# Two head groups whose cross-attention tiles alternate in the last batch of a decoder layer

## The reference

```python
x = x + self_attention(layernorm(x))          # 16 heads of 32, q and k layer-normed per head, causal
x = x + cross_attention(layernorm(x), ctx)    # 16 heads of 32
x = x + ffn(layernorm(x))                     # 512 -> 2048 -> 512
```

```python
scores = jnp.einsum('bhsd,bhnd->bhsn', Q, K) / SCALE
topk_scores, topk_indices = jax.lax.top_k(scores, 32)
sparse_weights = jax.nn.softmax(topk_scores, axis=-1)
context = sum(sparse_weights * V[topk_indices])
```

## Time and profile before

| | us |
|---|---|
| median of 3 timed runs | 3785.44 (3781.98 to 3794.32) |
| profiled execution, its own time | 3774.83 |
| its span, first to last instruction | 3773.0 |

### The profile page before, as it was taken

How to read it: one execution, slowest core, us unless ns; L and a number is a source line. 1 busy time by engine, 2 the same in 40 slices (tenths; PEclk the granted TensorE clock), 3 DMA queues, 4 the chain that set the end, 5 groups by cost and what they waited for, 6 DMA issues and landing times.

```text
span 3773.0 us, 60458 instructions
## 1 busy us (share of the span) xinstructions
PE 3260.6 (86%) x18118; PEld 2386.4 (63%) x18118; DVE 3229.3 (86%) x7622; ACT 2400.5 (64%) x4849; POOL 1924.7 (51%) x2444
## 2 busy tenths in 40 slices
PE   4887988998999988998999989998999989777765
PEld 2655776666676666666676766666666766455532
DVE  3441999999999998999899999999899998999951
ACT  2544666666776776667776777677666766555533
POOL 2232344466554665465654665466655654355445
PEclk8678788889998899889998899889899888887778
DMA  5323223221232223221232223322222222111100
GB/s 196 92 79 92 76 72 81 74 67 56 80 94 81 73 73 91 76 72 49 76 92 76 73 82 85 84 73 59 69 78 72 68 62 68 54 43 37 34 23 20
DMA packets 149985, 273.54 MB, mean 72 GB/s; under 512 B 39328, under 2 KB 39328, under 8 KB 148384
## 3 DMA queue, kind: packets, MB, share of 16 engines
q1 hardware_dynamic: 149664, 269.69, 25.4%
HBM read 106.98 MB, written 28.31 MB: 36 GB/s over the span
## 4 chain that ended last, share of the span: by engine, by line
PE 35%; DVE 34%; POOL 11%; issue 7%; ACT 7%; SPq 4%; DMA 2%; DVEq 0%; POOLq 0%; ACTq 0%
DVE cW L943 15%; DVE top L936 12%; PE bank L731 8%; PE bank L645 6%; PE bank L697 5%; SPq L520 4%; PE bank L631 3%; PE bank L715 3%; POOL srs L1281 2%; PE bank L750 2%; POOL hh L1245 2%; PE bank L673 2%; POOL hh L1249 2%; DVE smx L1073 2%; PE bank L743 2%
## 5 line engine op out<-in xcount | busy, mean ns | idle before, releaser
L943 DVE MATCH_REPLACE8 cW<-top,cW 128x512 f32<-128x512 f32 x1536 | 1026.1, 675 | 0.0
L936 DVE MAX8 top<-cW 128x8 f32<-128x512 f32 x1536 | 980.6, 680 | 0.0
L1302 POOL TENSOR_TENSOR cS<-cS,cW 128x512 f32<-128x512 f32 x512 | 642.5, 1277 | 204.7 <-ACT cW L873 204.2
L845 ACT ACTIVATE PT<-bank 128x512 f32<-128x512 f32 (+3 forms) x1024 | 538.1, 526 | 310.4 <-PE bank L631 307.3
L645 PE MATMUL bank<-cv,PT 128*128 128x33 f32 x4096 | 589.9, 291 | 123.3 <-ACT PT L845 122.5
L645 PEld LDWEIGHTS bank<-cv,PT 128*128 128x128 f32 x4096 | 558.7, 211 | 159.1 <-ACT PT L845 153.1
L1309 POOL TENSOR_SCALAR cnb<-top 128x2 f32<-128x2 f32 x256 | 49.4, 193 | 879.7 <-DVE top L936 860.5
L645 PEld LDWEIGHTS bank<-sv,PT 128*128 128x128 f32 x2560 | 397.9, 211 | 81.0 <-ACT PT L845 59.1
L873 ACT ACTIVATE cW<-cW,cnb 128x512 f32<-128x512 f32 x512 | 348.2, 735 | 137.2 <-DVE cW L943 137.0
L731 PE MATMUL bank<-w_group,xT 128*128 128x384 f32 x1024 | 413.5, 553 | 0.0
L867 ACT ACTIVATE cS<-cS,cnb 128x512 f32<-128x512 f32 x512 | 379.8, 742 | 43.9 <-POOL cnb L1309 24.6
(11 more groups left out here) (177 smaller groups left out, 5968.8 us busy)
## 6 DMA issues: line engine op xcount, KB each, us to landing
sk_stack<-part SPq DMA_DIRECT2D x512, 64.0 KB, 2.0
sq_stack<-part SPq DMA_DIRECT2D x512, 64.0 KB, 2.0
ck_stack<-part SPq DMA_DIRECT2D x512, 64.0 KB, 2.0
cq_stack<-part SPq DMA_DIRECT2D x512, 64.0 KB, 2.0
w_group<-in_wc SPq DMA_DIRECT2D x32, 768.0 KB, 4.3
w_group<-wa_by_group SPq DMA_DIRECT2D x28, 768.0 KB, 5.4
feed<-in_x SPq DMA_DIRECT2D x32, 256.0 KB, 3.0
ctxT<-in_ctx_t SPq DMA_DIRECT2D x8, 1024.0 KB, 5.6
```

The source lines that it names most:

```text
L845: act.activation(PT[k][:, 0:n], turned_ps[k][:, 0:n], ACT.Copy).then_inc(turned_read, step("turned_read", label))
L936: dve.max(top8[:, j, r, :], src[:]).then_inc(topk, step("topk", (c, r, "max", j)))
L943: dve.match_replace(cW[j][:], top8[:, j, r, :], src[:], REPLACED).then_inc(topk, step("topk", (c, r, "replace", j)))
L1302: pool.tensor_tensor(cS[m % 2][j][:], cS[m % 2][j][:], cW[j][:], ALU.subtract).then_inc(cprob, step("cprob", (m, j)))
```

## The change

In the last batch, cross items 120 to 127 no longer run group 30 with tiles 0 to 3 and then group 31 with tiles 0 to 3. They alternate: 30 tile 0, 31 tile 0, 30 tile 1, 31 tile 1, and so on. Since both groups are then in use at once, group 31's keys and queries go into the self attention's stacks, which have no more use, and they are made in slot 139 (cells 2 and 3) rather than in slot 142. Its weights are loaded in slot 138 rather than 141; `cross_v` of group 31 stays in slot 141. A row tile's output units follow its own last item: `cross_tile` comes at s = 144, 146, 148 and 150 for tiles 28 to 31 (before 147 to 150), `x2_tile` one slot later each. The MLP of the last batch begins at s = 146 (before 149), and LAST is 158.

```diff
-FIRST, LAST = -7, SLOTS * (NB - 1) + LAG + 29
+FIRST, LAST = -7, SLOTS * (NB - 1) + LAG + 26
+def cross_place(n):
+    b, r = divmod(n, SLOTS)
+    if b == NB - 1 and r >= SLOTS // 2:
+        t, k = divmod(r - SLOTS // 2, 2)
+        return NG * b + 2 + k, t
+    return n // NT, n % NT
+
+def cross_last(t):
+    b, qt = divmod(t, NT)
+    return SLOTS * b + (9 + 2 * qt if b == NB - 1 else SLOTS - NT + qt)
 def cross_tile(s):
-    return tile_at(s, LAG + 15)
+    return next((t for t in range(NTILES) if cross_last(t) + 3 == s - LAG), None)
 def x2_tile(s):
-    return tile_at(s, LAG + 16)
+    return cross_tile(s - 1)
 def mlp_step(s):
-    b, at = divmod(s - (LAG + 17), SLOTS)
+    last = SLOTS * (NB - 1) + LAG + 14
+    b, at = (NB - 1, s - last) if s >= last else divmod(s - (LAG + 17), SLOTS)
     g = cross_group(s)
     if g is not None:
         for at, cell, unit in ((1, 5, ("cross_v", g)), (2, 0, ("cross_kT", g)), (2, 3, ("cross_qT", g))):
-            if at == q:
+            if at == q and (unit[0] == "cross_v" or g != NGROUPS - 1):
                 u[cell].append(unit)
+        if q == 3 and g == NGROUPS - 2:
+            u[2].append(("cross_kT", g + 1))
+            u[3].append(("cross_qT", g + 1))
-                          + [(NT * g + LAG - 3, "cross", g) for g in range(NGROUPS)])
+                          + [(NT * min(g, NGROUPS - 2) + LAG - 3 + g // (NGROUPS - 1), "cross", g) for g in range(NGROUPS)])
@@ copy_part
-                        sp.wait_ge(score_full, upto("score_full", (which, NT * u[1] - 1, j)))
+                        used = (which, NT * u[1] - 1, j)
+                        if u[0].startswith("cross") and u[1] == NGROUPS - 1:
+                            stack, used = stack_of["self" + u[0][5:]], ("self", NS - 1, j)
+                        sp.wait_ge(score_full, upto("score_full", used))
@@ scores
-                        qt = n % NT
+                        g, qt = (n // NT, n % NT) if which == "self" else cross_place(n)
...
-                            pe.matmul(ps[:], cq_stack[:, j, qt * P:(qt + 1) * P], ck_stack[:, j, :], start=True,
+                            q_st, k_st = (cq_stack, ck_stack) if g != NGROUPS - 1 else (sq_stack, sk_stack)
+                            pe.matmul(ps[:], q_st[:, j, qt * P:(qt + 1) * P], k_st[:, j, :], start=True,
@@ unit, cross_oT
-                            pe.wait_ge(co_norm, upto("co_norm", SLOTS * (u[1] // NT) + SLOTS - NT + u[1] % NT))
+                            pe.wait_ge(co_norm, upto("co_norm", cross_last(u[1])))
```

More of the change, by code:

```diff
@@ L643, in values @@
                         o = out_of(which, m)
+                        g = m // NT if which == "self" else cross_place(m)[0]
                         for k in range(n):
                             mm = pe.matmul(o[:, j * (HD + 1):(j + 1) * (HD + 1)], pt[:, k * P:(k + 1) * P],
-                                           v[m // NT % len(v)][:, k, j, :], start=k == 0, stop=k == n - 1)
+                                           v[g % len(v)][:, k, j, :], start=k == 0, stop=k == n - 1)
                         if j == HG - 1:
@@ L660, in scores @@
                             for kind in ("kT", "qT"):
-                                copied(pe, (which + "_" + kind, n // NT), (j,))
+                                copied(pe, (which + "_" + kind, g), (j,))
                         if which == "self":
@@ L964, in norms @@
                                 continue
-                            b, qt, g = n // SLOTS, n % NT, n // NT % NG
+                            g, qt = (n // NT, n % NT) if k == 0 else cross_place(n)
+                            b, g = divmod(g, NG)
                             if b and g == 0:
```

## The result

| | before | after |
|---|---|---|
| median of the timed runs | 3787.9 us (5 runs) | 3765.2 us (5 runs, 3759.7 to 3768.7) |
| ratio, 95% interval | | 0.994 (0.9927 to 0.9953) |
| profiled execution: span | 3773.0 us | 3762.6 us |
| start of slot 139 | 3426.1 us | 3441.1 us |
| slots 139 to 142 | 93.5 us | 92.2 us |

The medians differ by 22.7 us; the forecast was 24.8. The two spans differ by only 10.4 us, because this execution reached slot 139 15.0 us later, in a part of the program that the change doesn't touch. From slot 139 on it is 25.4 us shorter.

What follows compares the result with a forecast made beforehand. DVE bounds the search slots, then a serial tail of 143.9 us follows. Terms -27.0 - 4.3 + 6.5 + 0 = -24.8 us, against the median of 3785.4 us a forecast of 3760.6 us, range 3746 to 3779 us.

Steps and rivals of the forecast that it cites:

- Steps 1 and 2: Tail after the search end: one MLP tile fewer, -27.0 us, and slots 148 to 151 shorter, -4.3 us.
- The walk of slots 148 to 151: Timing of norms and hmx after the search end with the new slot contents: gain 4.3 us.
- the ends given: Bounds on the worth of the MLP tile leaving the tail: 26.3 and 28.4 us around 27.0.
- Step 3: Search slots 144 to 147: DVE gets extra cross_rows, row scale and hmx work, +6.5 us, upper end 12.
- Step 4: Group 31's stack pair moves: slot 142 loses a 4.9 us stall, slot 139 gains the same, sum 0.
- new stall of the 4.8 us kind: Rival: late silu in slot 146 or late copies in slot 140; three stalls make -10.4 us, 3775 us; chance 0.14.
- The stacks: Rival: group 31's stacks land late, DVE idles over 34 us from slot 141, 3797 us or more; chance 0.04.
- POOL's load: Rival: 14 us of moved POOL work blocks DVE in full, -10.8 us, 3774.6 us; chance 0.02.
- The better case: Rival: slot 139 has no stall, about -30 us, 3755 us; chance 0.11.

Runs made afterwards that it cites:

- e1_mlp_late: The changed kernel with the MLP of the last batch beginning at slot 149 as before the change: median 3778.1 us, ratio 0.9968 to the kernel before.
- c1: The changed kernel run once more with no edit: median 3758.6 us, ratio 0.9921 to the kernel before.
- c2: The changed kernel run again with no edit, beside a rerun of the kernel before: median 3758.8 us, ratio 0.9914.
- e3: The changed kernel with POOL's early silu ahead of low_parts of cross_qT in slot 139 alone: median 3756.2 us, ratio 0.9907 to the kernel before.
- e4: The kernel before with POOL's early silu ahead of low_parts of cross_qT in slot 142 alone: ratio 0.9986 to the kernel before.
- e6: The changed kernel with 16 more POOL multiplications, 20 us, in slots 144 to 147: median 3761.8 us, ratio 0.9927 to the kernel before.

## Why the prediction was right, step by step

**Direction and size.** -24.8 us forecast; -22.7 us in the first comparison, -25.4 us in the stage of the first pair of traces, about -32 us in the two later comparisons. The forecast of 3760.6 us lies between the medians seen (3758.6 to 3765.2).

**Steps 1 and 2, the tail:** -31.3 us forecast, -30.0 measured. e1_mlp_late shows the cause: give the tile back and 19.9 us of the stage come back. The walk of slots 148 to 151 held: norms 3.3 us later, forecast and measured; first hmx 26.3 us after the search end forecast, 26.1 measured; fourth 41.8 and 42.6. The last is the one error, 0.8 us: x2t of tile 31 came at 31.2 us after the search end, and the third chunk behind it at 36.7 where the walk had 35.8. Gain 3.7 us in place of 4.3. The tile taken out was worth 26.4 us in this trace (54.7 us for two that stay of 81.05), within the ends given.

**Step 3, DVE work in the search slots:** +6.5 us forecast, +6.0 in the first trace, +6.7 in c1 and c2. Slot by slot 24.1, 22.2, 23.4, 23.6 forecast, 24.0, 22.1, 23.2, 23.5 measured. What varied is cross_rows' wait for PE in slot 146, 0.6 and 1.3 us.

**Step 4, the pair of group 31:** 0 forecast; -1.3 in the first pair of traces, -0.1 for c1 and c2 against the first trace of the kernel before, -1.6 against its second. One term was mis-sized. Slot 139's stall was 3.0 us and not 4.9: the walk put hmx 22.1 us into the slot, it came at 20.4 (3461.53 - 3441.13), because the second low_parts began 15.5 us into slot 139, where it had begun 17.4 us into slot 142. So the move of the pair is worth 1.8 us (4.8 gone, 3.0 come). Slot 142 did fall by its whole stall, to 21.8 us and the norms' wait of 0.4 to 1.7 us. That the sum came out near 0 is luck: the only trace of the kernel before that the prediction had was one in which the norms of slot 142 did not wait; in its second trace they waited 1.4 us. The queue itself (hmx behind silu behind low_parts behind PE) was named rightly: e3 takes it out of slot 139 and 3.1 us go, e4 out of slot 142 and 4.9 us go against the trace with the same wait of the norms.

**Rivals.** No new stall of the 4.8 us kind in slots 140 to 147. The stacks were not late. In the trace after, the last copy of head 0's queries landed at 3461.4 us and PE's first score with them began at 3464.0; the last copy of all landed at 3475.2, and PE's score of head 3 began at 3479.6. DVE took the first of these scores with slot 141, at 3488.5 us. (The sum of that rival was off: -24.8 and 34 us of idle make 3794.6 us; for its 3797 us DVE would have to idle over 36.) POOL's load costs DVE nothing (e6). The better case, no stall in slot 139, did not come by itself; one line of order brings it.

## What to carry to other kernels

When a pipeline ends in a serial tail, ask which item of work makes its first unit complete, and reorder the last round so that units complete one after another while the bound engine still has work; the price is what the moved work puts on that engine, here 6 us for 30. Before a slot is priced to a microsecond, take a second trace of the same kernel: here one slot of one program had a wait of 1.4 us in one trace and none in the other, and against a single trace such a wait looks like a result of the change. In an in-order queue, a piece that others wait for should not stand behind one that waits for a far engine, but only where nothing else is late next: the same turn gave 3 us in one slot and nothing in seven batches.

## What the runs showed of the hardware

TensorE's granted clock made most of what differed between two executions of one program from slot 139 on. The down product of a tail tile, the same 16 matmuls, shows it. At a granted clock of 1.00 over the product, the level of 2.4 GHz, it takes 3.61 us, and the tile 26.3 us. At 0.63 to 0.68, part of it at the level of 1.2 GHz, it takes 5.2 to 5.7 us, and the tile 27.9 to 28.4 us, in either kernel. PE had done the same before both: it waited 7.2 us for POOL, then transposed for 3.8 us at a granted clock of 0.50. Which tile of a run got the slow one changed from run to run. And a DVE search of 512-wide rows, 677 ns for a MATCH_REPLACE8, is untouched by 19.7 us of two-input POOL multiplications beside it.
